# A second wait ahead of each group of gathers in a recommendation tower

## The reference: what is computed

```
gram = einsum('bfd,bgd->bfg', all_emb, all_emb)      # all_emb: 2048 x 27 x 128
z = gram[:, _TRIU_I, _TRIU_J]                        # the pairs above the diagonal
h = concatenate([z, r_bottom_output], axis=1)        # 479 numbers
h = maximum(h @ W_top1 + b_top1, 0)                  # 512
h = maximum(h @ W_top2 + b_top2, 0)                  # 256
y = h @ W_top3                                       # 1
```

## Time and profile before

| | |
|---|---|
| median of 3 runs | 498.77 us |
| lowest and highest | 496.91 and 505.03 us |
| span of the profiled execution | 370.7 us |
| own time of the profiled execution | not given |
| what lies around the span, by the median | 128.1 us |
| mean granted TensorE clock in the profile | 0.963 of full speed |

### The profile page before, as it was taken

How to read it: one execution, slowest core, us unless ns; L and a number is a source line. 1 busy time by engine, 2 the same in 40 slices (tenths; PEclk the granted TensorE clock), 3 DMA queues, 4 the chain that set the end, 5 groups by cost and what they waited for, 6 DMA issues and landing times.

```text
span 370.7 us, 8525 instructions
## 1 busy us (share of the span) xinstructions
PE 343.2 (93%) x3422; PEld 282.3 (76%) x3422; DVE 236.3 (64%) x312; ACT 230.8 (62%) x298; POOL 257.2 (69%) x261
## 2 busy tenths in 40 slices
PE   6899999999699999999999999997977996899996
PEld 5688888887587778788788877776866785677886
DVE  2999999999497769798789945313340332522452
ACT  2699989888497896499997833447321473223222
POOL 5777878777777777777877877777777777770010
PEclk9699999999699999999999999999896999899999
DMA  6977687665957789988767629534593425323200
GB/s 174 249 217 211 194 248 222 190 198 163 319 112 251 205 242 341 287 235 252 230 156 245 191 77 347 176 96 114 152 366 99 115 74 146 97 52 85 66 20 2
DMA packets 48391, 66.86 MB, mean 180 GB/s; under 512 B 15861, under 2 KB 34847, under 8 KB 47840
## 3 DMA queue, kind: packets, MB, share of 16 engines
q1 hardware_dynamic: 40024, 49.32, 43.9%
q0 software_dynamic: 8064, 16.31, 16.7%
q10 hardware_dynamic: 264, 0.69, 0.6%
HBM read 52.36 MB, written 13.93 MB: 179 GB/s over the span
## 4 chain that ended last, share of the span: by engine, by line
PE 69%; POOL 10%; DMA 6%; ACT 5%; issue 5%; DVE 3%; SPq 1%; ACTq 0%; DVEq 0%
PE acc L624 21%; PE acc L625 21%; POOL rows L591 10%; PE gram L655 9%; PE turned L637 6%; PE acc L660 4%; PE acc L661 4%; PE acc L662 4%; DMA rows<-in_tbl,index 2%; DMA wanted<-in_onehot_ids 2%; DVE onehot L899 2%; ACT features L741 1%; ACT staged L823 1%; ACT h L769 1%; DMA square<-products 1%
## 5 line engine op out<-in xcount | busy, mean ns | idle before, releaser
L591 POOL DMA_INDIRECT rows<-in_tbl,index x248 | 253.9, 1024 | 77.7 <-issue 74.4
L899 DVE TENSOR_SCALAR onehot<-wanted,row_number 125x1029 fp32r<-125x1029 int32 (+3 forms) x137 | 151.0, 1150 | 19.6 <-PE acc L625 13.3
L624 PE MATMUL acc<-onehot,table_hi 125*128 125x512 f32 x336 | 136.6, 407 | 3.1 <-DVE table_lo L893 3.1
L625 PE MATMUL acc<-onehot,table_lo 125*128 125x512 f32 x288 | 115.7, 402 | 0.0
L624 PEld LDWEIGHTS acc<-onehot,table_hi 125*128 125x128 f32 x336 | 64.7, 193 | 17.8 <-DVE table_lo L893 3.3
L655 PEld LDWEIGHTS gram<-features 128*54 128x54 f32 x2048 | 60.6, 136 | 17.6 <-issue 14.6
L655 PE MATMUL gram<-features 128*54 128x52 f32 x2048 | 67.5, 222 | 6.0 <-DVE features L925 3.0
L625 PEld LDWEIGHTS acc<-onehot,table_lo 125*128 125x128 f32 x288 | 55.7, 194 | 12.4
L769 ACT ACTIVATE h<-wanted,row_number 125x1029 f32<-125x1029 int32 x42 | 48.8, 1163 | 23.4 <-PE acc L625 20.3
L637 PE MATMUL turned<-identity,rows 128*128 128x128 f32 x248 | 41.8, 294 | 9.9 <-DMA rows<-in_tbl,index 8.1
L772 ACT ACTIVATE onehot<-h,row_number 125x1029 fp32r<-125x1029 f32 x42 | 48.6, 1157 | 1.4
(11 more groups left out here) (49 smaller groups left out, 285.4 us busy)
## 6 DMA issues: line engine op xcount, KB each, us to landing
wanted<-in_onehot_ids SPq DMA_DIRECT2D x20, 514.5 KB, 6.0
parked<-staged SPq DMA_DIRECT2D x32, 256.0 KB, 4.3
table_raw<-in_tbl SPq DMA_DIRECT2D x17, 448.0 KB
looked<-parked SPq DMA_DIRECT2D x2, 2816.0 KB, 12.4
square<-products SPq DMA_DIRECT2D x62, 84.5 KB
rows<-in_tbl,index POOLq DMA_INDIRECT x248
looked<-parked SPq DMA_DIRECT2D x1, 2560.0 KB, 11.0
pairs<-in_tbl SPq DMA_DIRECT2D x3, 448.0 KB
```

The lines of the kernel that those rows point to most:

```text
L591: pool.indirect_dma_start(out=rows[:, n % ROWS_RING, i, :], out_offset=None, in_=gathered[f], in_offset=bass.IndirectOffsetOnAxis(ap=index ...
L624: pe.matmul(to, table_hi[0:ROW_PARTS, v % HIGH_RING, c, :], of, start=(c == 0), stop=False)
L625: last = pe.matmul(to, raw_table(v, low=True)[0:ROW_PARTS, c, :], of, start=False, stop=(c == CHUNKS - 1))
L899: return dve.tensor_scalar(column[:, rows], ids_of(v, slice(0, ROW_PARTS))[:, rows], row_number[0:ROW_PARTS, c:c + 1], None, ALU.is_equal)
```

## The change

`order()` now also computes, for each group of gathers, which lookup or chunk it has to wait for. It notes at each turn when the group would begin by the planner's clock (`gathered` minus `GATHER_LANDS`, 3.8 us), and takes the last lookup or chunk that has ended, by the same clock, at least `PACE_LEAD` (10 us) before that. POOL waits for this step ahead of the group, besides the wait for the ring. For the first five groups there is none.

```diff
+GATHER_LANDS = 38
+PACE_LEAD = 100
...
     steps, now, gathered = [], 0, GATHER_START
     grams = 0
+    begins, ended, paces = [], [], []
 
     def turn():
         nonlocal now, gathered
         step = turns.pop(0)
+        begins.append(gathered - GATHER_LANDS)
         gathered += groups_of(step[1])[step[2]] * GATHER_LENGTH
...
         grams += step[0] == "gram"
-    return steps
+        if step[0] in ("lookup", "gram"):
+            ended.append((now, step))
+    for begin in begins:
+        paces.append(max(((end, step) for end, step in ended if end <= begin - PACE_LEAD), default=(0, None))[1])
+    return steps, paces
...
-ORDER = order()
+ORDER, PACES = order()
...
+            def keep_pace(n):
+
+                if PACES[n] is None:
+                    return
+                kind, x, y = PACES[n]
+                if kind == "lookup":
+                    pool.wait_ge(accumulated, visited(x))
+                else:
+                    pool.wait_ge(grammed, x * TILE_CHUNKS + y + 1)
...
                     at_least(pool, transposed, n - ROWS_RING + 1)
+                    keep_pace(n)
                     for i in range(size):
```

## The result

| | median | lowest to highest | runs |
|---|---|---|---|
| before | 498.17 us | 496.91 to 505.03 | 4 |
| after | 474.78 us | 463.57 to 488.91 | 4 |

The change is faster: ratio 0.932, 95% interval 0.919 to 0.945. This ratio leaves out the disturbed runs, those over 1.5% above the fastest of their kernel, here 481.37 and 488.91 us after; the medians of all runs, 474.78 and 498.17 us, give 0.953. My forecast of no change, 495 to 504 us, was wrong.

The account below looks back on a forecast made before the run. PE's stream of work, busy 343.2 of 370.7 us, was taken to bound the kernel, with POOL's gathers close behind. Span 370.7 + 0 for the waits, with 128.1 us around it, gave 498.8 us, range 495 to 504.

Parts of the forecast that it names:

- the term for the hold: POOL, heads of the 59 paced groups: each awaited step is done before the group starts, so waits cost 0.
- the 128.1 us that lie around the span: Whole execution: time outside the profiled span, taken from the median of the runs and added to 370.7 us.
- My slack of 5.3 to 26.9 us: POOL, 59 group heads: time from the awaited step's end to the group's first gather, 5.3 (group 60) to 26.9 us (group 16).
- the sign: POOL, before group heads: idle stretches of a microsecond and more would mean the forecast is wrong and PE runs later.
- What a fulfilled wait takes: POOL, 42 second waits by group 50: taken as 0, with an upper bound of 2.9 us put into the range.
- The first rival: POOL, group heads: a second wait is its own instruction costing 0.07 us; 501.7 us in all; chance 0.15.
- the last: POOL, group heads: a second wait drains POOL and costs 0.30 us, 12.6 us by group 50; 511.4 us; chance 0.05.
- The rival of relief: DMA engines: pacing relieves them and removes up to 8.1 us of PE's waits for rows; 490.7 us; chance 0.03.
- The rivals of 495.1 and 511.4 us: Group 50's gathers fall ahead of the `looked` load, saving 3.70 us; second waits drain POOL, costing 12.6 us; chance 0.05 each.

Follow-up runs that it names:

- e1: The kernel before, unchanged, run again for a second profile: 374.09 us, ratio 0.999 to before at 373.57 us.
- e4: The change with a lead of 30 us instead of 10: 374.37 us, ratio 0.997 to before at 373.57 us.
- e3: The change with a lead of 0 instead of 10 us: 376.03 us, ratio 1.008 to before at 373.57 us.
- e14: The change with its waits aimed at indices that landed long before, so they never hold POOL: 506.56 us, ratio 1.002 to before at 506.63 us.
- e2: The change with its waits aimed at indices that landed long before, so they never hold POOL: 374.72 us, ratio 1.003 to before at 373.57 us.
- e8: The kernel before, unchanged, run once more: 374.77 us, ratio 1.009 to before at 374.25 us.
- e11: The kernel before with only the first gather of each group (64 of 248), PE's work kept: 356.13 us beside before at 374.25 us.
- e17: The kernel before with only the first gather of each group (64 of 248), PE's work kept: 358.98 us, ratio 0.718 to before at 502.06 us.
- e18: The change with a lead of 0 instead of 10 us: 466.97 us, ratio 0.931 to before at 503.82 us.
- e15: The kernel before with only the first gather of each group (64 of 248), PE's work kept: 356.17 us beside before at 373.94 us.
- e13: The kernel before with only the first gather of each group (64 of 248), PE's work kept: 356.53 us beside before at 374.68 us.
- e16: The change with a lead of 0 instead of 10 us: 374.22 us, ratio 1.005 to before at 373.94 us.
- e5: The change, unedited, timed again against the kernel before: 472.94 us, ratio 0.933 to before at 504.79 us.
- e7: The change with each lookup's high product made twice on PE: 495.81 us beside the kernel before at 504.79 us.

## Why the prediction was wrong

**The step that failed is the term for the hold: "So no wait holds POOL. This term is 0."** I read it from a profile of the 374 condition, and the runs were made in the 500 one. The sum should have shown me this. It took "the 128.1 us that lie around the span by the median of the runs", and they don't lie around the span: 1.8 us do (468.20 against 466.4, and 374.2 against 372.4 in e1). The other 126.3 us, a quarter of the time, were inside the timed executions and not in my profile, and I explained the difference instead of doubting the profile. By itself this error moved nothing, since the 128.1 us stood in the sum before and after alike; it let the slack stand.

**What the runs showed in its place.** For the 374 condition the term was right: e4 with its weaker hold and e3 with a stronger one give the time of before. In the 500 condition PE falls behind its plan early. The waits for chunks and lookups hold POOL for 49.7 us (45.1 and 4.6), and the first of them, at group 5, already for 3.13 us, to 32.07; the group 45 of the rows above starts at 296.39, just after its step. My slack of 5.3 to 26.9 us was used up. And this hold is a gain: with the same instructions and no hold the time is that of before (e14, 1.002), with it the ratio is 0.93. The text had named the sign ("PE runs later against POOL in other executions than in this one") but given it no place in the sum, since I priced it as a loss at most.

**What a fulfilled wait takes** was right, and could be tested apart: 0, by e2, whose heads have 0.30 us before them like all others. The first rival, 0.07 us each, and the last, 0.30, fall with it. The Trainium skill's page "Perfetto Trace Analysis" (Identifying Dependency Chains) is confirmed by the page of the profile: 8580 instructions instead of 8525, one for each of the 55 second waits. The 50 to 100 ns that the Trainium skill's page "Advanced Engine Details and Errata" (Miscellaneous Facts) gives for reading a semaphore don't appear in POOL's spacing (0.305 us before heads with two waits and inside groups alike).

**The rival of relief** had the right sign and the wrong mechanism. I looked for DMA engines that gathers would crowd, and capped its price by the waits for transfers, 8.1 us. What the gathers hinder is PE: its short matmuls come one to five at a time, and what it has finished is seen late. In e14 ACT stands still as well. No wait of the earlier trace rows could show this, since that profile has none of it.

**The rivals of 495.1 and 511.4 us** did not decide: nothing in the runs calls for the phase of the `looked` load, and no second wait drained POOL.

**What stays open.** What sets the condition is not known. It stayed the same within each comparison, and the chip with number 10 was in the one condition with e8 to e11 and in the other with e17, so it isn't simply a property of that number. Why a hold by PE's steps helps more than the ring's is open in part: e14 and the change have 36 pauses of POOL each, of 123 and 114 us in all, and yet lie 37 us apart. The long streams are fewer in the change (its longest are 20 gathers, e14's is 44), but e18 has one of 60 and is as fast, so this isn't the whole answer. That in the 500 condition a signal given during a gather is seen only after it is shown by e17 and e15, and that the gathers cost the time by e17; e17 changes their number and their spacing at once, and all 248 gathers spaced singly were not tried. By what path POOL's gathers hold back the other engines' signals was not tried either.

## What to carry to other kernels

Where a profile's span and the timed runs lie far apart (here 370.7 and 498.77 us, with 1.8 us around a span), the profile may be of another condition, and no slack read from it should be used before that is settled. Time an edit in every condition that the kernel meets: leads of 0 and 30 us were worth nothing at 374 us, and leads of 0 and 10 us were worth 7% at 500. Where gathers issued by POOL run beside PE, compare the end of a PE step with the start of the one who waits for it, once while POOL gathers and once while it is held.

## What the runs showed of the hardware that I had not expected

- The same kernel ran in 374 us or in 500 us and nothing between: in 374 beside e1 to e4, e8 to e13, e15 and e16, in 500 in the first comparison and beside e5 to e7, e14, e17 and e18.
- In the 500 condition a finished chunk was seen 2.7 us late in the mean while POOL gathered, and 0.08 us late while it did not; the longest single delay that a row above shows is 7.1 us. In the 374 condition it was seen 0.02 us late in the mean while POOL gathered.
- Beside single gathers of 0.94 us, in the 500 condition, 29 of 30 chunks that ended inside one were seen only after its end, 0.7 to 1.3 us late, and this cost next to nothing: 358.98 against 356.17 us.
- In the 500 condition the kernel took 143 us longer with 248 gathers in streams than with 64, most of them single with pauses between them; in the 374 condition 18 us.
